# A routed expert kernel on one core: how the block of engine programs is closed

## What is computed

```python
xn = rms_w * (x * jax.lax.rsqrt(var + EPS))
gate = xn @ wg_W + wg_b + (genre_embed @ gg_W + gg_b)
gate_w = jax.nn.softmax(gate, axis=-1)
topk_w, topk_i = jax.lax.top_k(gate_w, TOP_K)
...
h1 = jax.nn.relu(jnp.einsum('bsh,ehm->bsem', x, W1) + b1)
h2 = jax.nn.relu(jnp.einsum('bsem,emn->bsen', h1, W2) + b2)
out_e = jnp.einsum('bsen,enh->bseh', h2, W3) + b3
return jnp.einsum('bseh,bse->bsh', out_e, cw)
```

## Time and profile before

| what | value |
|---|---|
| median of three executions | 464.17 us |
| lowest and highest | 463.86 and 465.04 us |
| span of the profiled execution, first to last instruction of the program | 461.3 us |
| PE busy | 423.9 us (92% of the span) |
| Pool busy | 305.3 us (66%) |

### The profile page before, as it was taken

The page is one execution under the profiler, slowest core; times in us unless marked ns, Lnnn a source line. Parts: engine busy times, 40 slices in busy tenths (PEclk is TensorE's granted clock), DMA queues, the critical chain, the costliest instruction groups (busy, mean ns, idle before and its releaser), DMA issues.

```text
span 461.3 us, 13037 instructions
## 1 busy us (share of the span) xinstructions
PE 423.9 (92%) x4252; PEld 381.7 (83%) x4252; DVE 307.7 (67%) x539; ACT 289.0 (63%) x609; POOL 305.3 (66%) x457
## 2 busy tenths in 40 slices
PE   7606999999999999999999999999999999989980
PEld 6506988988999988999899999889999899979880
DVE  4799774877667577577577577555566667756650
ACT  6604949878687777787786675444444556655550
POOL 5632853778788878788778887876555666464361
PEclk9955899999999999999999999999999999999995
DMA  8989299456445434232243332342333332011231
GB/s 303 343 240 349 97 342 339 129 156 157 133 67 139 139 59 132 47 62 37 48 120 75 65 54 24 72 70 49 50 51 45 47 50 49 14 26 29 26 36 19
DMA packets 27178, 49.46 MB, mean 107 GB/s; under 512 B 8267, under 2 KB 21645, under 8 KB 24941
## 3 DMA queue, kind: packets, MB, share of 16 engines
q0 software_dynamic: 13632, 18.00, 24.0%
q1 hardware_dynamic: 9280, 30.45, 18.5%
q10 hardware_dynamic: 4205, 0.17, 0.5%
HBM read 40.08 MB, written 17.83 MB: 126 GB/s over the span
## 4 chain that ended last, share of the span: by engine, by line
PE 77%; DVE 7%; ACT 4%; DMA 2%; issue 2%; POOL 1%; another core or an unknown queue 0%; DVEq 0%; SPq 0%; POOLq 0%; ACTq 0%
PE bank L1295 51%; PE y_banks L1376 18%; PE bank L1255 3%; PE bank L1280 3%; DMA stage<-in_weights 2%; ACT area L800 2%; DVE area L1092 1%; PE bank L1164 1%; PE y_banks L1243 1%; DMA out<-area,cto 1%; DVE area L1090 1%; POOL out L638 1%; ACT area L824 1%; DVE stage L1117 1%; ACT w_hi L738 0%
## 5 line engine op out<-in xcount | busy, mean ns | idle before, releaser
L1295 PE MATMUL bank<-area,w_hi 128*128 128x256 f16 x1536 | 253.8, 273 | 0.3 <-issue 0.2
L1295 PE MATMUL bank<-area,w_lo 128*128 128x256 f16 x768 | 209.3, 273 | 0.0
L814 ACT ACTIVATE area<-bank,cprm 128x256 f32<-128x256 f32 (+1 forms) x264 | 131.0, 557 | 55.4 <-PE bank L1295 47.3
L1295 PEld LDWEIGHTS bank<-area,w_hi 128*128 (+1 forms) x1536 | 150.1, 98 | 17.9 <-issue 0.7
L638 POOL DMA_INDIRECT out<-area,cto x71 | 121.6, 1713 | 45.3 <-issue 21.0
L1090 DVE CAST area<-area 128x512 f16<-128x512 f32 (+1 forms) x144 | 68.0, 472 | 118.6 <-ACT area L814 105.7
L1092 DVE TENSOR_TENSOR area<-area 128x512 f16<-128x512 f32 (+1 forms) x144 | 100.8, 700 | 5.0
L603 POOL DMA_INDIRECT area<-x_ext,cfrom x65 | 72.0, 1107 | 37.9 <-POOL cfrom L598 27.9
L1376 PE MATMUL y_banks<-w_hi,area 128*128 (+1 forms) x520 | 90.7, 273 | 2.8 <-DVE area L1092 2.8
L1295 PEld LDWEIGHTS bank<-area,w_lo 128*128 (+1 forms) x768 | 75.1, 98 | 8.7
L824 ACT ACTIVATE area<-area,cw 128x256 f32<-128x256 f32 x71 | 32.2, 499 | 71.4 <-DVE area L1097 50.6
(11 more groups left out here) (205 smaller groups left out, 458.9 us busy)
## 6 DMA issues: line engine op xcount, KB each, us to landing
stage<-in_weights SPq DMA_DIRECT2D x10, 1024.0 KB
area<-in_x SPq DMA_DIRECT2D x8, 512.0 KB, 7.2
x_ext<-in_x SPq DMA_DIRECT2D x8, 512.0 KB
out<-in_x SPq DMA_DIRECT2D x8, 512.0 KB
w_lo<-in_weights SPq DMA_DIRECT2D x4, 1024.0 KB
w_hi<-in_weights SPq DMA_DIRECT2D x2, 1024.0 KB
out<-area,cto POOLq DMA_INDIRECT x71
area<-x_ext,cfrom POOLq DMA_INDIRECT x65
```

What stands on the lines that cost most here:

```text
L814: ins = act.activation(to[:, m * T + u * wide:m * T + (u + 1) * wide], ps_h[layer][b][:, a * T + u * wide:a * T + (u + 1) * wide], ACT.Rel ...
L1295: ins = nc.tensor.matmul(banks[m // 2][:, (m % 2) * T:(m % 2) * T + wide], weight, xp[:, cols], start=(k == 0 and n == 0), stop=(k == chun ...
```

## The change

The block is opened with one more argument:

```diff
-        block = ctx.enter_context(nc.Block())
+        block = ctx.enter_context(nc.Block(no_gpsimd_drain=True))
```

## The result

| | kernel before | changed kernel |
|---|---|---|
| median of four executions each | 464.01 us | 460.20 us |
| lowest and highest | 463.84 and 465.04 us | 459.02 and 460.73 us |
| span of the profiled execution | 461.3 us | 457.3 us |

The ratio is 0.9901, with an interval of 0.9880 to 0.9923: 1.0% faster, 3.8 us by the medians.

What follows compares the result with a forecast made beforehand. The prediction took the kernel as PE-bound, its end as Pool's series. Span 461.3 - 4.37 = 456.9 us, plus 2.9 us around it, gave 459.8 us (0.94% faster), range 459.0 to 462.8 us.

Steps and rivals of the forecast that it cites:

- The bound and its place: Whole kernel PE-bound, PE busy 92% of the span; but the program's end is a series with Pool alone in it.
- the missing 6.9 us of the chain: Between the chain's stop at 454.39 us and the span's end at 461.3 us; to be sought among sequencers' instructions.
- The term of 4.37 us: End barrier: Pool's drain of 4.32 us and some 0.05 us to the next instruction go, all on the path.
- The landing as the next late thing: End of Pool's program: the wait for the last addition's landing, at 456.5 us, is late next; no new wait appears.
- The 2.9 us around the span: Outside the program: median device time lies 2.9 us over the profiled span, assumed to stay as it is.
- Rival one: Behind the span: the launcher's closing steps drain Pool instead, 4.3 us return, 464.1 us, no change; chance 0.15.
- Rival two: Behind the program's end: 0.9 to 3.0 us of the drain's time return, giving 460.7 to 462.8 us; chance 0.06.
- Rival three: Next execution's first gather meets unsettled descriptors; price unknown, measurably slower from 5.8 us on; chance 0.03.
- Rival four: End barrier: Pool's semaphore instruction waits as the drain did, so the change does nothing, 464.2 us; chance 0.01.

Runs made afterwards that it cites:

- the last experiment: Kernel before with both edits at once: a Pool drain added in tile 33, where Pool idles, and Pool's last wait for additions removed; ratio 0.9915.
- two drains: Kernel before with one more Pool drain directly ahead of the end barrier's own; ratio 1.0007.
- one drain under cover: Kernel before with one more Pool drain in tile 33, where Pool is idle waiting for ACT; ratio 0.9926.

## Why the prediction was right

**The bound and its place.** That the end of the program is a series with Pool alone in it, and that the missing 6.9 us of the chain were to be found among sequencer instructions, held wherever the last wait stands. An edit forecast at 0.9% stood in no row of working instructions. The prediction's answer to what the drain waits for, "not for transfers", is right for this place, where all had landed; the last experiment shows a drain that waits for a landing.

**The term of 4.37 us.** Shown by the drain put back (4323 ns, ratio 1.0007) and by the semaphore instruction that follows the branch at once (457.0 to 457.1 us, 17 ns). I had taken zero for what that instruction might inherit, and the rows agree. That the debt came from 71 additions and 71 gathers was right in kind only: the 4323 ns settle some 51 DMAs' worth, not 142. Measured on the medians, the gain is 3.8 us in both comparisons rather than 4.37, with intervals from 2.4 to 5.6 us over the two; the 4.1 us between the run with the drain put back (1.0007) and the changed kernel (0.9919) is the same quantity once more. Whether the half microsecond is real can't be said from these.

**The landing as the next late thing.** Held: the wait ends at 457.0 us in the changed kernel, and the last addition's 1.56 us of generating and 2.2 us of landing are as before.

**The 2.9 us around the span.** Mis-sized. I took it from a span of one execution and a median of three others. With both numbers from the same executions it is 1.6 to 1.8 us, before and after. The profiled execution of before had simply been one of the faster, 461.3 us where spans reach 465.1; with 1.6 to 1.8 us added it comes to some 463 us, under the lowest of the four in the table. The error cancelled, because the forecast was in effect the median less 4.37 us; that the time came out within 0.4 us of the forecast owes nothing to this term. It had a second effect: the forecast of the span, 456.9 us, was made as if PE's part were fixed, and it was 457.3 in the profiled execution and 457.5 to 460.8 in six others.

**Rival one**, the moved drain, was given 0.15 and is refuted for this launcher by the constant difference between device time and span. The rule named beside it (the Trainium skill, "VectorE: DVE Perf Modes", section "The DRAIN you can't avoid": drains of some 12 ns on all five engines around the program) is neither confirmed nor refuted, since no row here shows such a drain. If one follows on Pool, it doesn't pay the debt in the measured time. My reason for the rival, that a drain depends on what Pool has generated since the last one, was right, and the inference from it was not.

**Rival two**, a part that comes back, finds no row: the branch and the semaphore instruction stand 0.2 us apart, and the launcher's part is unchanged. Its price of 0.9 to 3.0 us had come from no row either, and the range's upper end of 462.8 us rests on it. **Rival three**, the debt found by the next execution, would have lengthened the first gather, which took 1.39 us as before, or the drain in the start barrier, which took 172 ns. I had overlooked that this drain comes before the gather. How the next execution gets a clean start without settling isn't seen in any row. **Rival four** fell with the missing drain.

## What to carry to other kernels

When the chain of waits ends well ahead of the span, look at the sequencer instructions behind it: barriers and drains are counted as neither busy nor idle. A Pool that issues indirect DMAs runs up a debt that the next drain pays, on the path where nothing else runs beside it. Leave that drain out where a wait for the landings already stands at the end, or put one where Pool is idle for 4 us anyway. Don't put it right behind a transfer, where it waits for the landing too. And take span and device time from the same executions before adding what lies around the span.

## What the runs showed of the hardware

- A drain of Pool costs some 40 ns plus 83 ns for each indirect DMA of 128 rows issued and not settled yet (2 in 0.21 us, 5 in 0.46, 6 in 0.57, 10 in 0.90, 12 in 1.03, 64 in 5.3; 36 in 3.0, where a landing may have a part), although all had landed. At the same place of the program the value repeats exactly: 4323 ns in the profiles of three kernels (before, drain put back, two drains), 3915 ns in two (one drain under cover, both at once).
- The settling starts when Pool's last instruction ends, runs beside landings, isn't done by itself while Pool works on something else for 5.2 us or is idle for 9.3, and the drain that had little to settle didn't end before the landing had (2.3 us behind generating).
- Without any drain the debt doesn't grow to 142. By the price of 83 ns it was 51 DMAs at the end, and it fell on the way (60 at the 98th, 32 at the 122nd); why stays open.
- Executions of one kernel differ by up to 4 us in their span (461.1 to 465.1 us for the kernel before), as much as the whole effect here, while the launcher's part stays at 1.63 to 1.82 us, with and without a drain of Pool at the end. Only the kernel with 36 drains has more, 2.07 to 2.11 us; why isn't known.
